# The last six steps of a two-layer cross-attention kernel: flat instruction lists, the last y^T by TensorE, the last layer norm on VectorE

## What is computed

```python
# layer 0
Q = x @ Wq0 + bq0;  K = ctx @ Wk0 + bk0;  V = ctx @ Wv0 + bv0
y = x + softmax(Q @ K.T / sqrt(512), axis=-1) @ V @ Wo0 + bo0
# layer 1, with the softmax over the query rows
q = y @ Wq1 + bq1;  k = ctx @ Wk1 + bk1;  v = ctx @ Wv1 + bv1
w = softmax(q @ k.T / sqrt(512), axis=query rows)
z = y + w @ v
out = (z - mean(z)) / sqrt(var(z) + 1e-6) * gamma + beta
```

## Time and profile before

| | us |
|---|---|
| median of 3 runs | 1189.31 (1188.04 to 1190.63) |
| the profiled execution | 1189.45 |
| its span | 1187.7 |

### The profile page before, as it was taken

One profiled execution on the slowest core, in us unless ns is written; L12 is line 12 of the kernel. 1 busy time (PEld: TensorE's weight loads), 2 busy tenths in 40 slices (PEclk: granted clock), 3 DMA queues, 4 the chain that ended last, 5 costly groups with the idle time before them and its releaser, 6 DMA issues.

```text
span 1187.7 us, 25309 instructions
## 1 busy us (share of the span) xinstructions
PE 1153.1 (97%) x7992; PEld 1074.9 (91%) x7992; DVE 891.2 (75%) x2074; ACT 859.2 (72%) x1736; POOL 967.5 (81%) x772
## 2 busy tenths in 40 slices
PE   9989999999999999999999999999999999999983
PEld 7879999999999999999999999999999999999873
DVE  2667787777778777787877877787787777778763
ACT  2557777777777777777777777777777777777652
POOL 2458898898889889888888988988898898889764
PEclk9999999999999999999999999999999999999997
DMA  8555666676666666666666666666666666666431
GB/s 322 174 166 210 221 222 218 212 238 199 226 224 219 218 210 234 199 229 227 218 217 212 229 206 227 228 215 217 215 224 211 222 228 210 225 217 218 152 115 54
DMA packets 132127, 250.09 MB, mean 211 GB/s; under 512 B 15744, under 2 KB 89472, under 8 KB 123648
## 3 DMA queue, kind: packets, MB, share of 16 engines
q1 hardware_dynamic: 131088, 248.64, 62.0%
q10 hardware_dynamic: 1008, 1.06, 0.3%
HBM read 165.68 MB, written 83.95 MB: 210 GB/s over the span
## 4 chain that ended last, share of the span: by engine, by line
PE 96%; DVE 2%; ACT 1%; POOL 0%; issue 0%; DMA 0%; SPq 0%; POOLq 0%; DVEq 0%; ACTq 0%
PE bank L329 91%; PE bank L407 2%; PE bank L441 1%; PE bank L448 1%; PE bank L468 1%; DVE scol L894 0%; DVE stats L915 0%; ACT bank L551 0%; DMA gT<-g_dram 0%; POOL Y L1133 0%; DVE R L907 0%; DVE w_lo L882 0%; SPq L243 0%; ACT Y L685 0%; ACT bank L659 0%
## 5 line engine op out<-in xcount | busy, mean ns | idle before, releaser
L1077 POOL TENSOR_TENSOR yT_lo<-yT_raw,yT_hi 128x1024 fp32r<-128x1024 f32 x64 | 152.3, 2380 | 26.1 <-ACT yT_hi L551 24.7
L1077 POOL TENSOR_TENSOR xT_lo<-IN,xT_hi 128x1024 fp32r<-128x1024 f32 x64 | 154.4, 2413 | 22.2 <-ACT xT_hi L551 22.2
L1133 POOL TENSOR_TENSOR Y<-Y,gamma_b 128x512 f32<-128x512 f32 x128 | 162.9, 1295 | 0.9 <-ACT Y L685 0.9
L1136 POOL TENSOR_TENSOR Y<-Y,beta_b 128x512 f32<-128x512 f32 x128 | 163.2, 1297 | 0.0
L685 ACT ACTIVATE Y<-R,nmr,rstd 128x512 f32<-128x512 f32 x128 | 97.5, 809 | 79.3 <-POOL nmr L1125 79.3
L1123 POOL TENSOR_TENSOR rstd<-ve,half 128x2 f32<-128x2 f32 x64 | 44.8, 701 | 134.2 <-DVE nmu L930 134.2
L329 PE MATMUL bank<-yT_hi,A_hi 128*128 128x256 f32 x512 | 144.4, 282 | 2.1 <-issue 1.1
L329 PE MATMUL bank<-xT_hi,A_hi 128*128 128x256 f32 x512 | 144.4, 282 | 1.1 <-DVE A_lo L934 1.1
L329 PE MATMUL bank<-xT_hi,A_lo 128*128 128x256 f32 x512 | 144.4, 282 | 0.0
L329 PE MATMUL bank<-yT_lo,A_hi 128*128 128x256 f32 x512 | 144.2, 282 | 0.0
L329 PE MATMUL bank<-xT_lo,A_hi 128*128 128x256 f32 x512 | 144.0, 281 | 0.0
(11 more groups left out here) (114 smaller groups left out, 4236.6 us busy)
## 6 DMA issues: line engine op xcount, KB each, us to landing
IN<-in_packed SPq DMA_DIRECT2D x64, 1024.0 KB, 4.9
R<-in_x SPq DMA_DIRECT2D x64, 512.0 KB, 4.3
y_dram<-y_blk SPq DMA_DIRECT2D x256, 128.0 KB, 2.6
yT_raw<-y_dram SPq DMA_DIRECT2D x64, 512.0 KB, 3.5
out<-Y SPq DMA_DIRECT2D x64, 512.0 KB, 2.6
E_dram<-E_blk SPq DMA_DIRECT2D x256, 64.0 KB, 1.8
PT_raw<-E_dram SPq DMA_DIRECT2D x64, 256.0 KB, 2.7
gT<-g_dram SPq DMA_DIRECT2D x64, 128.0 KB, 3.8
```

The source lines that it names most:

```text
L1077: return nc.gpsimd.tensor_tensor(dst, src, fp(hi), ALU.subtract)
L1133: nc.gpsimd.tensor_tensor(y[:, q, :], y[:, q, :], gamma_b[:, :], ALU.mult).then_inc(Y_mul, 1)
L1136: last = nc.gpsimd.tensor_tensor(y[:, q, :], y[:, q, :], beta_b[:, :], ALU.add)
```

## The change

`spread` is `stats_ready` and `variances`. The new functions:

```diff
+            def yT_last(q):                                            # TensorE
+                if q == 0:
+                    pe.wait_ge(ident_set, 1)
+                    pe.wait_ge(u_lo, T(3).count(2, 1))
+                else:
+                    pe.wait_ge(g_set, T(3).count(2, 1))
+                pe.wait_ge(x1_set, T(3).count(2, q))
+                for d in range(DT):
+                    last = nc.tensor.transpose(bank[2 + q][:, d * P:(d + 1) * P], R[T(3).k % 4][:, q, d * P:(d + 1) * P],
+                                               ident[:, :])
+                last.then_inc(yT_last_full, 1)
+            def s_last():
+                pe.wait_ge(s_set, T(2).count())
+                pe.wait_ge(w_lo, T(3).count())
+                parts = [w[a][:, t, :] for a in range(2) for t in range(ST)]
+                for t, part in enumerate(parts):
+                    last = nc.tensor.matmul(s_bank[:, 0:S], ones[:, :], part, start=(t == 0), stop=(t == 3))
+                last.then_inc(s_full, 1)
+            def pred_last(q):
+                if q == 0:
+                    pe.wait_ge(wc_lo, T(3).count())
+                product(bank[2 + q][:, :], lambda a, t: wcT[a][:, t, q * P:(q + 1) * P],
+                        lambda b, t: V1[b][:, t, :], LT).then_inc(pred_full, 1)
+            def yT_last_h():                                           # ScalarE
+                act.wait_ge(v_full, T(2).count())
+                for q in range(ST):
+                    act.wait_ge(yT_last_full, q + 1)
+                    copy(yT[0][:, q * DT:(q + 1) * DT, :].rearrange("p a b -> p (a b)"), bank[2 + q][:, :]
+                         ).then_inc(yT_last_hi, 1)
+            def yT_last_l():                                           # VectorE
+                for q in range(ST):
+                    dve.wait_ge(yT_last_hi, q + 1)
+                    last = minus(yT[1][...], bank[2 + q][:, :], yT[0][...])
+                last.then_inc(yT_lo, 1)
+            def add_s(q):
+                y = R[T(3).k % 4][:, q, :]
+                dve.wait_ge(s_set, T(3).count())
+                nc.vector.scalar_tensor_tensor(y, bv1_b[:, :], scol[:, q, 0:1], y, ALU.mult, ALU.add
+                                               ).then_inc(s_added, 1)
+            def x2_last(q):
+                y = R[T(3).k % 4][:, q, :]
+                dve.wait_ge(pred_full, T(3).count(2, q))
+                dve.wait_ge(s_added, q + 1)
+                nc.vector.tensor_tensor(y, bank[2 + q][:, :], y, ALU.add).then_inc(x2_set, 1)
+            def finish_last():
+                y = R[T(3).k % 4]
+                dve.wait_ge(mv_set, T(3).count())
+                for q in range(ST):
+                    nc.vector.scalar_tensor_tensor(y[:, q, :], y[:, q, :], nmu[:, q:q + 1], gamma_b[:, :], ALU.add,
+                                                   ALU.mult).then_inc(centred, 1)
+                dve.wait_ge(y_out[1], 16 * (NSEQ // 2 - 1))
+                dve.wait_ge(norm_step, T(3).count())
+                for q in range(ST):
+                    dve.wait_ge(centred, q + 1)
+                    nc.vector.scalar_tensor_tensor(Y[1][:, q, :], y[:, q, :], rstd[:, q:q + 1], beta_b[:, :], ALU.mult,
+                                                   ALU.add).then_inc(Y_last, 1)
+            def scales_last():                                         # GpSimd
+                pool.wait_ge(mv_set, T(3).count())
+                pool.wait_ge(Y_set, T(2).count(2, 1))
+                nc.gpsimd.tensor_tensor(rstd[:, :], ve[:, :], half[:, :], ALU.pow).then_inc(norm_step, 1)
+            def store_last():                                          # SP
+                for q in range(ST):
+                    sp.wait_ge(Y_last, q + 1)
+                    sp.dma_start(o_v[T(3).index()][:, q * D:(q + 1) * D], Y[1][:, q, :]).then_inc(y_out[1], 16)
```

More of the change, by code:

```diff
@@ L31, in __init__, with ends @@
         self.k, self.base = k, base
+    def ends(self):
+        return self.base is None and self.k >= NSEQ - 4
     def plus(self, d):
@@ L82, in build @@
         half = sb("half", [P, ST])
+        ident = sb("ident", [P, P])
         WqT0_s = sb("WqT0_s", [P, HT, D])
@@ L317, in _ @@
                     body(Seq(LOOP_FROM + k, j))
-            for r in range(LOOP_FROM + 4 * LOOP_TRIPS, NSEQ + 2):
+            for r in range(LOOP_FROM + 4 * LOOP_TRIPS, NSEQ - 4):
                 body(Seq(r))
+            load_x(T(2))
+            write_g(T(1))
+            store(T(-2))
+            read_g(T(1))
+            write_E0(T(3))
+            load_x(T(3))
+            write_y(T(2))
+            read_E0(T(3))
+            store(T(-1))
+            read_y(T(2))
+            write_g(T(2))
+            read_g(T(2))
+            write_g(T(3))
+            read_g(T(3))
+            store(T(0))
+            store(T(1))
+            store(T(2))
+            store_last()
             sp.wait_ge(y_out[0], 16 * (NSEQ // 2))
-            sp.wait_ge(y_out[1], 16 * (NSEQ // 2))
+            sp.wait_ge(y_out[1], 16 * (NSEQ // 2 + 1))
         @block.tensor
@@ L667, in w_h @@
                 first(act, wc_full, n.count(back=1))
+                if n.ends():
+                    act.wait_ge(s_full, n.count(back=1))
                 for m in range(ST):
@@ L783, in _ @@
                     body(Seq(LOOP_FROM + k, j))
-            for r in range(LOOP_FROM + 4 * LOOP_TRIPS, NSEQ + 1):
+            for r in range(LOOP_FROM + 4 * LOOP_TRIPS, NSEQ - 4):
                 body(Seq(r))
+            wc_h(T(-1))
+            C_h(T(3))
+            pred_seed_(T(-1))
+            PT_h(T(2))
+            u_h(T(3))
+            out_seed_(T(2))
+            yT_h(T(1))
+            Pc_h(T(2))
+            exps1(T(0))
+            exps0(T(3))
+            w_h(T(0))
+            normalise(T(-1))
+            S1_seed_(T(1))
+            v_h(T(1))
+            wc_h(T(0))
+            pred_seed_(T(0))
+            PT_h(T(3))
+            exps1(T(1))
+            w_h(T(1))
+            out_seed_(T(3))
+            Pc_h(T(3))
+            yT_h(T(2))
+            wc_h(T(1))
+            S1_seed_(T(2))
+            normalise(T(0))
+            pred_seed_(T(1))
+            v_h(T(2))
+            yT_last_h()
+            exps1(T(2))
+            w_h(T(2))
+            S1_seed_(T(3))
+            v_h(T(3))
+            wc_h(T(2))
+            normalise(T(1))
+            pred_seed_(T(2))
+            exps1(T(3))
+            w_h(T(3))
+            wc_h(T(3))
+            normalise(T(2))
         @block.vector
@@ L1070, in _ @@
                     body(Seq(LOOP_FROM + k, j))
-            for r in range(LOOP_FROM + 4 * LOOP_TRIPS, NSEQ + 1):
+            for r in range(LOOP_FROM + 4 * LOOP_TRIPS, NSEQ - 4):
                 body(Seq(r))
+            wc_l(T(-1))
+            dot(T(1), 0)
+            dot(T(1), 1)
+            g_blocks(T(1))
+            u_l(T(3))
+            x2(T(-1), 0)
+            x2(T(-1), 1)
+            moments(T(-1))
+            spread(T(-1))
+            Pc_l(T(2))
+            max1(T(0))
+            max0(T(3))
+            rz1_(T(0))
+            E0_blocks(T(3))
+            w_l(T(0))
+            x1(T(2), 0)
+            x1(T(2), 1)
+            y_blocks(T(2))
+            dot(T(2), 0)
+            dot(T(2), 1)
+            v_l(T(1))
+            s_columns(T(0))
+            wc_l(T(0))
+            g_blocks(T(2))
+            max1(T(1))
+            x2(T(0), 0)
+            rz1_(T(1))
+            x2(T(0), 1)
+            w_l(T(1))
+            moments(T(0))
+            Pc_l(T(3))
+            spread(T(0))
+            s_columns(T(1))
+            x1(T(3), 0)
+            wc_l(T(1))
+            x1(T(3), 1)
+            dot(T(3), 0)
+            dot(T(3), 1)
+            g_blocks(T(3))
+            v_l(T(2))
+            yT_last_l()
+            max1(T(2))
+            x2(T(1), 0)
+            rz1_(T(2))
+            w_l(T(2))
+            x2(T(1), 1)
+            moments(T(1))
+            spread(T(1))
+            v_l(T(3))
+            s_columns(T(2))
+            wc_l(T(2))
+            max1(T(3))
+            rz1_(T(3))
+            x2(T(2), 0)
+            w_l(T(3))
+            x2(T(2), 1)
+            moments(T(2))
+            s_columns(T(3))
+            wc_l(T(3))
+            spread(T(2))
+            add_s(0)
+            add_s(1)
+            x2_last(0)
+            moments_last(0)
+            x2_last(1)
+            moments_last(1)
+            spread(T(3))
+            finish_last()
         @block.gpsimd
```

74 lines of the change are left out of this document (72 added, 2 removed).

## The result

The changed kernel takes 1173.56 us (median of 4 runs, 1172.65 to 1174.09), the kernel before 1188.67 beside it (4 runs, 1187.17 to 1190.63): ratio 0.9868, 95% interval 0.9855 to 0.9880. The profiled execution took 1174.09, with a span of 1172.3.

What follows compares the result with a forecast made beforehand. Loop bound by TensorE's own work; only the drain can move. TensorE ends at 1124.8 + 31.7 work + 6.1 gaps = 1162.6; with the tail the span is 1174.4, plus 1.75 gives 1176.1 us; range 1173.2 to 1181.5.

Steps and rivals of the forecast that it cites:

- PE's 1124.8: Start of the drain sum: the time from which TensorE's 31.7 us of work and 6.1 of gaps were added.
- point 3: Drain, gap before S1(62): transposes fill 0.9 of 1.9 us, 1.0 idle; removed DRAM trip worth its old 1.0, no more.
- 1174.4: Forecast end of the span in us, after the tail and 1.9 for the shared SBUF ports.
- 1.75: Time around the span in the profiled execution of before, 1189.45 - 1187.7, added to the forecast span.
- rival C: Tail, less is lost: ports cost nothing and half stores land 0.6 sooner; 1173.6 to 1174.2 us, chance 0.10.
- step 2: Drain, gaps before Pc(63) and wc(61): E0 read lands in 2.7 us, TensorE idles 0.3 in both together.
- rival B: Drain, ScalarE queue held by transfers: g lands in 6.5, E0 in 4; 1179 to 1181 us, chance 0.12.
- 31.7 us: TensorE's work left in the drain: 30.7 in the old order, plus 0.12 for s_last and 0.9 for eight transposes.
- rival A: Half clock stays in the drain: one stretch gives 1177.7 us, two give 1179.3; chance 0.27.
- D: Rival: half clock holds through the drain from the gap before S1(61) on, slower than before, 1202 us; chance 0.03.
- The port term: Tail: VectorE instructions with two SBUF operands and GpSimd wait for each other; 1.9 us, bounds 0 and 2.6.
- The halves: Tail, last store in two halves: saves little; the second's issue and landing take 2.5 to 3.1 us, 3.1 used.

Runs made afterwards that it cites:

- e4: Changed kernel with y^T(63) written to and read from DRAM again, no transposes on TensorE: 1182.95 us, ratio 0.9947 to the kernel before.
- e0: Changed kernel again with no edit, for a second profile: 1174.23 us, ratio 0.9876 to the kernel before.
- e1: Kernel before with only the identity tile and the two GpSimd instructions that fill it: 1188.39 us, ratio 0.9998.
- e2: Changed kernel with read_E0(63) ahead of write_y(62) in SP's list: 1172.32 us, ratio 0.9862 to the kernel before.
- e8: Changed order of all engines with the old operations (y^T(63) through DRAM, seeded prediction, old layer norm, one store, s(63) behind wc(63)): 1186.55 us, ratio 0.9988.
- e9: Changed kernel with gamma and beta copied to PSUM and read there by VectorE's last four instructions: 1173.49 us, ratio 0.9851 to 0.9888.
- e7: Kernel before in its own order, with only y^T(63) made by TensorE transposes behind pred(61): 1189.82 us, ratio 1.0004.
- e6: Changed kernel with the last prediction seeded by ScalarE as before, without VectorE's add_s: 1173.67 us, ratio 0.9879 to the kernel before.
- e5: Changed kernel with the old layer norm for sequence 63 (ScalarE's normalise, finish on GpSimd, one store): 1178.08 us, ratio 0.9906 to the kernel before.
- e10: Changed kernel with read_E0(63) first, seeded last prediction, gamma and beta in PSUM, earlier last power, store(62) between the last halves: 1172.73 us, ratio 0.9866.

## Why the prediction was right or wrong

Two steps of the prediction failed. One is the term that the sum starts from: PE's 1124.8, with u(63) at 1107.46, read from a single execution. The changed kernel's u(63) began at 1104.77, and at 1105.4 in the mean of all other profiles, 2.1 to 2.7 us earlier; that is nearly all of the 2.5 by which the number was too high. The other is a mechanism, point 3's "worth its old 1.0 of idle, and no more": putting the trip through DRAM back cost 7.5 to 8.2 us (e4). That one did not show in the sum, which was made in the new order.

The length of the drain came out right, 1174.4 - 1107.46 = 66.9 us, measured 67.5 and 66.9 (e0), in part by luck: see the tail.

**The base.** I summed against one profiled execution, whose u(63) began at 1107.46. Over the other twelve profiles of this study it begins at 1105.4 in the mean. The range took in the doubts of the drain and none of this one. With 1105.4 the same sum gives 1105.4 + 66.9 + 1.75 = 1174.1, against 1173.56 and 1174.23. The gain was forecast 1.9 too small for the same reason seen from the other side: before's own profile joined a late start to a short drain (80.24; 81.67 in e1), so that its total looked like the median. That the time fell into rival C's bounds is no point for C: the half stores did land 0.6 sooner, but the ports cost 1.3.

**PE's gaps.** On the forecast's clock (2.69 added to the times of after) PE ended at 1164.8 and not at 1162.8. The gaps, forecast and measured:

| in front of | forecast | measured |
|---|---|---|
| S1(61) | 1.0 | 0.62 |
| pred(60) | 0.3 | 0.06 |
| Pc(63), wc(61) | 0.3 | 1.62 |
| S1(62), around the transposes | 1.0 | 0.70 |
| pred(62) | 1.2 | 0.98 |
| s_last | 0.65 | 0.50 |
| pred_last | 1.65 | 1.41 |
| sum | 6.1 | 5.9 |

The places were right, and so was the sum, by one error against six small ones. The one is step 2: the landing of PT_raw(63), 4.05 instead of the median 2.7. I had it as rival B, whose condition ("E0 in 4") came true for its second half; in the other runs with this order the gap is 0.70 to 1.40, with landings of 3.24 to 3.92, and without the gap the drain is 1.3 to 1.9 shorter (e2). What made PE late is another term, which I had not seen: the groups' own time, 31.7 us (31.9 with the last latency) where it measured 34.1. I took pred at 2.77 and S1 at 1.43, which are times from start to start of groups that follow without a stop. A group between two stops takes 3.04 (pred(62): 1151.93 to 1155.47 less 0.50 of idle) and 1.69 (S1(61): 1122.91 to 1124.66 less 0.06): 0.27 more. The rows show both ends of it: the last product runs to its own end, which in a row lies under the next group, and the first takes 0.39 where the later ones of 256 columns take 0.28. Over all stops of the drain that comes to some 2.0, of which I had 0.2 at the very end. The transposes took 0.60 and 0.66, 1.3 with both latencies, against 0.9. So 1.8 + 0.4 - 0.2 (the gaps) = 2.0.

**Half clock.** None came back in the changed kernel's drain (rival A's chance of 0.27, D's 0.03): its longest idle piece is 1.62. In the drains the runs agree with the forecast's reading of before: in e4 and e8 the pieces of 2.9, 3.7 and 1.93 were followed by a fall, those of 1.0 and 1.4 not. But 1.93 is not the shortest: the half clock of before at 71 us follows a piece of 1.85 that the forecast had missed, and so does e9's. One and the same piece can also go either way. The 1.93 ahead of the last prediction was followed by half clock in e1, e7 and e8 and not in before, the 2.15 ahead of pred(62) in before and e1 and not in e7, and at 70 us the 1.87 of the changed kernel and the 2.20 of e1 not. So it is in part luck that none came back here. The Trainium skill, "TensorE: Matmul & The Clock Gate", Part 4, gives some 275 ns for a transpose (bfloat16, in one kernel) and says that it does not count as work for the clock. Here four of float32 end after 0.60 us, and the granted clock stays at 1.00 around them; with 0.7 us of idle beside 1.3 of transposes the whole hole is 2.0, and no run tells whether they kept the clock.

**Point 3.** The places and times of the transposes were right; "worth 1.0 and no more" was wrong, by e4: 7.9. Its parts: 3.7 idle at v(63), 1.6 of half clock in it, 1.1 more between v(62) and S1(62), 1.5 of half clock behind that: 7.9. I had priced the removed trip by the wait that it caused in the old order. There the transposes gain nothing that the runs resolve (e7). In the new order v(63) comes earlier against its source, and the trip would be what is late.

**The tail.** As described: finish(62) on GpSimd ends last, then the power, then Y. The port term was 1.9 for 1.3: add_s held the power of 62 by 0.43, the centring held beta by 0.43 and the power of 63 by 0.44 (1.13, 2.93, 1.14 against 0.70, 2.49, 0.70 in e6 and e9). VectorE's own loss, 1.9 in the centring, lay beside finish(62) and cost nothing. The halves brought 0.6 where I had written that they save little. Sum for the drain: PE +2.0, ports -0.6, stores -0.6, nearly the +0.6 that the two traces give. Two errors, PE 2.0 too early and the tail 1.2 too long, largely cancelled: that is luck.

**What each part is worth.** Lists alone 1.0 to 2.4 us (e8 against before and e1; 2.3 by the medians), transposes alone nothing resolved (e7), identity 0 (e1); in the new order the transposes 7.5 to 8.2 (e4), the new layer norm 4.3 (e5), the last prediction without seed -0.8 to 0 (e6). The sum, lists 1.0 + 7.9 + 4.3 - 0.8 = 12.4, comes near the 12.7 between the two profiles, but that does not show that the parts add up. The place of s_last (2.0, e8 against e6) is in none of them, and the tail behind PE depends on when PE ends: 12.75 us in e8 and 14.53 in e5, with the same old layer norm.

**Where u(63) begins.** The profiles split it into two parts. The first u product starts anywhere from 17.45 to 19.72 us. From there to u(63) it takes 1086.7 to 1087.0 us in eleven of the thirteen profiles, and 1088.0 and 1088.1 in the two that have half clock at 71 to 75 us: before (0.58) and e9 (0.61). So a late start of the first product and at times one stretch of half clock are the whole of it. What sets the first product's start is open; nothing was tried for it.

## What to carry to other kernels

Price an operation in the order in which it will run: the transposes that gained nothing in the old order gained 7.9 us in the new one, and the new order with the old operations gained 1.0 to 2.4. When groups on TensorE get stops between them, add what a stop costs (0.27 us here) to times that were read from groups in a row. On one queue, put a read that someone waits for ahead of writes whose reader comes later. Set a sum not on one execution's absolute start but on the stretch that the change touches, and take that stretch from several profiles of before: its old drain took 80.24 in one and 81.67 in another.

## What was not expected of the hardware

A VectorE instruction of two elements per partition can wait for a whole GpSimd instruction. VectorE and GpSimd of the changed kernel, in order of time:

```profile
1132.65 2.40 POOL L1336 TENSOR_TENSOR yT_lo<-yT_raw,yT_hi 128x1024 fp32r<-128x1024 f32 x1 [1.06 <-ACT yT_hi L652]
1132.76 2.32 DVE L1079 TENSOR_SCALAR ve<-mv 128x2 f32<-128x2 f32 x1
1135.00 0.15 DVE L1080 TENSOR_SCALAR nmu<-mv 128x2 f32<-128x2 f32 x1
```

ve takes 0.17 at 1159.15 and 2.32 here, where it ends 0.03 after yT_lo; it has one input, so it is not only instructions with two that wait. (The Trainium skill, "SBUF — State Buffer", section "Who interferes with whom", names tensor_scalar among those that can take the shared pair; the trace agrees, and the forecast had looked only for two inputs.) In e6 and e10 it took 1.27 beside finish(62), in the very chain that sets the end. A read took 4.05 us to land behind four writes and 3.6 ahead of them, where 2.7 is the median. And two VectorE instructions that would take 1.41 took 3.31 when they alternated with GpSimd's, while GpSimd lost only 0.44: the loss is not shared equally.
